# A vision tower's attention: the scaling of the probabilities goes from GpSimd to VectorE, as two operations with a scalar for each row

## The reference, cut to what matters

```python
scale = HEAD_DIM ** (-0.5)
attn = jnp.einsum('bhqd,bhkd->bhqk', q, k) * scale
attn = attn + jnp.einsum('bhqd,qkd->bhqk', q, r_p_k) * scale
attn = jax.nn.softmax(attn, axis=-1)
out = jnp.einsum('bhqk,bhkd->bhqd', attn, v)
out = out + jnp.einsum('bhqk,qkd->bhqd', attn, r_p_v)
return out.transpose(0, 2, 1, 3).reshape(b, n, QKV_DIM) @ proj_w.T + proj_b
```

## Time and profile before

| | us |
|---|---|
| median of 3 runs (4234.64 to 4243.27) | 4240.48 |
| the profiled execution | 4242.51 |
| its span | 4240.8 |
| TensorE busy in it | 4025.1 (95%) |
| VectorE busy | 2885.2 (68%) |
| ScalarE busy | 2497.5 (59%) |
| GpSimd busy | 1280.7 (30%) |

### The profile page before, as it was taken

One profiled execution on the slowest core, in us unless ns is written; L12 is line 12 of the kernel. 1 busy time (PEld: TensorE's weight loads), 2 busy tenths in 40 slices (PEclk: granted clock), 3 DMA queues, 4 the chain that ended last, 5 costly groups with the idle time before them and its releaser, 6 DMA issues. The chain is left out here.

```text
span 4240.8 us, 84769 instructions
## 1 busy us (share of the span) xinstructions
PE 4025.1 (95%) x28203; PEld 3938.8 (93%) x28203; DVE 2885.2 (68%) x7468; ACT 2497.5 (59%) x6686; POOL 1280.7 (30%) x1423
## 2 busy tenths in 40 slices
PE   4986799999999999999999999999999799999999
PEld 4886699999999999999999999999999799999999
DVE  4675566766666766676766676667666677777776
ACT  2554666666766666666676666666665344444443
POOL 1323322232232232223223223222222344444443
PEclk8998899999999999999999999999999899999999
DMA  8641100000000000000000000000000322222222
GB/s 188 141 114 48 36 1 1 1 25 1 2 24 2 1 2 24 1 1 24 1 1 25 1 1 2 24 1 1 13 1 1 92 93 93 93 91 87 82 90 90
DMA packets 88974, 161.67 MB, mean 38 GB/s; under 512 B 5706, under 2 KB 75937, under 8 KB 85055
## 3 DMA queue, kind: packets, MB, share of 16 engines
q1 hardware_dynamic: 85118, 152.66, 12.6%
q0 software_dynamic: 944, 2.42, 0.3%
q10 hardware_dynamic: 2576, 2.36, 0.2%
HBM read 127.82 MB, written 29.60 MB: 37 GB/s over the span
## 5 line engine op out<-in xcount | busy, mean ns | idle before, releaser
L637 POOL TENSOR_TENSOR att_prob<-att_prob,att_total 99x396 f32<-99x396 f32 x768 | 649.9, 846 | 2108.7 <-DVE att_total L869 2108.7
L877 DVE TENSOR_REDUCE att_npeak<-att_s 99x2 f32<-99x396 f32 x768 | 434.8, 566 | 449.4 <-PE att_s L1090 440.5
L718 ACT ACTIVATE att_probT<-att_t 99x396 f32<-99x396 f32 x768 | 384.1, 500 | 572.1 <-PE att_t L1056 566.7
L730 ACT ACTIVATE att_prob<-att_s,att_npeak 99x198 f32<-99x198 f32 x1536 | 636.6, 424 | 137.3 <-DVE att_npeak L877 135.4
L1073 PE MATMUL att_o<-att_probT,att_vx 99*96 99x198 f32 (+1 forms) x3072 | 653.5, 335 | 1.1 <-DVE att_rx L862 1.1
L1090 PE MATMUL att_s<-att_kx,att_qx 96*99 96x198 f32 (+1 forms) x3072 | 642.5, 332 | 5.2 <-DVE att_qx L821 2.2
L1278 POOL TENSOR_TENSOR ffn_hidden<-ffn_relu 128x384 f32<-128x384 f32 x462 | 425.3, 927 | 482.6 <-ACT ffn_relu L1307 480.6
L1090 PEld LDWEIGHTS att_s<-att_kx,att_qx 96*99 96x99 f32 (+1 forms) x3072 | 481.4, 166 | 12.4 <-issue 6.0
L1307 ACT ACTIVATE ffn_relu<-ffn_h 128x384 f32<-128x384 f32 x462 | 225.7, 489 | 448.4 <-PE ffn_h L1527 446.5
L1539 PE MATMUL ffn_y<-ffn_down,ffn_hidden 128*128 128x192 f32 x2772 | 487.3, 327 | 1.6 <-DVE ffn_hidden L1431 1.6
L1073 PEld LDWEIGHTS att_o<-att_probT,att_vx 99*96 99x96 f32 (+1 forms) x3072 | 469.5, 179 | 4.4 <-issue 1.4
(11 more groups left out here) (241 smaller groups left out, 8117.8 us busy)
## 6 DMA issues: line engine op xcount, KB each, us to landing
ffn_gates<-gate_rows SPq DMA_DIRECT2D x66, 768.0 KB, 5.5
tok_pixels<-in_x SPq DMA_DIRECT2D x24, 1568.0 KB
ffn_hid<-hidden SPq DMA_DIRECT2D x35, 288.0 KB, 3.0
att_xres<-hidden SPq DMA_DIRECT2D x8, 1188.0 KB
hidden<-att_xres SPq DMA_DIRECT2D x8, 1188.0 KB
ffn_acc<-hidden SPq DMA_DIRECT2D x33, 288.0 KB, 2.9
out_hidden<-ffn_acc SPq DMA_DIRECT2D x33, 288.0 KB, 2.4
hidden<-tok_rows SPq DMA_DIRECT2D x7, 1176.0 KB
```

The lines of the kernel that those rows point to most:

```text
L637: nc.gpsimd.tensor_tensor(prob[:, i % 2, :, :], prob[:, i % 2, :, :], view(total[:, i % 2, :], [[1, 2], [0, NTOK]]), ALU.mult).then_inc(pr ...
L718: nc.scalar.activation(probT[:, i % 2, :], t_bank[0:HALF, 0:2 * NTOK], ACT.Copy).then_inc(probT_made, 1)
L730: ins = nc.scalar.activation(prob[:, i % 2, h, :], s_bank[i % 2][0:HALF, h * NTOK:(h + 1) * NTOK], ACT.Exp, bias=npeak[:, i % 2, h:h + 1], ...
L877: nc.vector.tensor_reduce(npeak[:, i % 2, :], s_bank[i % 2][0:HALF, 0:2 * NTOK].rearrange("p (h k) -> p h k", h=2), AX.X, ALU.max, negate= ...
```

## The change

GpSimd's multiplication of the probabilities by the reciprocals (one operation with two tensors, 99 x 396) is taken out. VectorE gets `scaled`: it waits for its own reciprocal of the head before, and multiplies each half of the tile, 99 x 198, by a scalar for each row. That stands in VectorE's step n behind `inverted_sums` and behind `put_out`, and ahead of the step's jobs. The second of the two operations counts `probs`. GpSimd still adds the bias in the first 16 steps of a group, and now waits for `probs` instead of `inverted`.

```diff
                 def group(g, s):
                     for i in range(STEPS):
-                        pool.wait_ge(inverted, g * STEPS + i + 1)
-                        nc.gpsimd.tensor_tensor(prob[:, i % 2, :, :], prob[:, i % 2, :, :],
-                                                view(total[:, i % 2, :], [[1, 2], [0, NTOK]]), ALU.mult).then_inc(probs, 1)
                         if i < TILES:
+                            pool.wait_ge(probs, g * STEPS + i + 1)
                             if i == 0:
                                 pool.wait_ge(norm_made, (g + 1) * TURN)
                             ins = nc.gpsimd.tensor_tensor(xres[:, s, i, :], xres[:, s, i, :], pbias[:, :], ALU.add)
...
+                def scaled(n, i):
+
+                    j = i - 1
+                    dve.wait_ge(inverted, n - 1 + 1)
+                    for h in range(2):
+                        ins = nc.vector.tensor_scalar(prob[:, j % 2, h, :], prob[:, j % 2, h, :], total[:, j % 2, h:h + 1], None, ALU.mult)
+                    ins.then_inc(probs, 1)
+
...
                             inverted_sums(n, i)
                         if v != "first" or i >= 3:
                             put_out(n, i)
+                        if v != "first" or i >= 1:
+                            scaled(n, i)
                         for j in spreads[v][i]:
                             job(base, g, s, v, *j)
...
                     if i == STEPS:
                         inverted_sums(n, i)
+                        scaled(n, i)
                     put_out(n, i)
```

## The result

| | before | after |
|---|---|---|
| median of 4 runs each, us | 4241.0 | 4334.5 |
| ratio of the runs' times | 1 | 1.0226 (95%: 1.0211 to 1.0242) |
| span of the profiled execution | 4240.8 | 4329.6 |
| TensorE busy | 4025.1 | 4050.1 |
| VectorE busy | 2885.2 | 3285.7 |

The change made the kernel 93.5 us slower by the medians, 2.2%. 4324 was forecast, with 4272 to 4352 as the range. GpSimd's work halved, VectorE's grew by 400 us, and both mattered only through TensorE, whose matmuls are the same.

What follows compares the result with a forecast made beforehand. TensorE was taken as the bound. Seven groups' 66.5 us and the last group's 16.5 made 83 us on the span of 4240.8, so 4324 us; the range of 8 in 10 was 4272 to 4352.

Steps and rivals of the forecast that it cites:

- steps 74 to 82: Steps of a group where the next tokens are turned and VectorE is already the bound: 2.8 us lost a group.
- The way of 0.635 us behind L862: Scaled tile ready 0.585 us behind L862's end, plus 0.05 to the weight load: transposes can start 0.635 behind it.
- VectorE's time of 0.53 a step: What VectorE's line loses each step to the two scalings: the middle between 0.47 and 0.58 us.
- Unit ends: Steps 12 to 15 and the ends at 28 and 60: 0.9 us of VectorE's time plus 0.44 later transposes, 1.35 each.
- 42 to 47: Steps where the next group's statistics stand too: 1.63 us idle against 3.2 added, plus 0.44, so 2.0 us lost.
- the tail: Last group's 17 final steps with hardly any jobs: seven lose 0.93 us each, five some 0.5 each, 9 us.
- rival A: VectorE's added time is absorbed, only the longer chain to the transposes counts: 4281 us, range 4266 to 4300; chance 0.18.
- seven groups of 9.5 us: Every group but the last loses 9.5 us over its listed stretches, 66.5 us in all.
- The floor of 2.9: Loop from transpose load over weighing and copies to scaling: 2.26 plus 0.635, 2.9 us a step where rows show 1.97.
- (D): The work stays hidden, VectorE's idle time is used everywhere: within 0.2% of 4240 us; chance 0.04.
- (B): Late jobs free banks late, the ring of four empties, ScalarE gets peaks late: 4345 to 4390 us; chance 0.14.
- (C): GpSimd's operation slows VectorE's while both run, so without it the kernel gets faster: 4210 us; chance 0.04.

## Why the prediction was right, point by point

- **What bounds the kernel.** TensorE, with VectorE in steps 74 to 82 alone. Both hold: taking VectorE work out moved just these steps, up to what the clock did at a group's end.
- **The removed part.** GpSimd's operation was no bound, only a way of 0.98 us. Right as far as the runs go: a longer way alone cost 85 us. No run takes the operation away without putting work elsewhere.
- **The two operations.** Forecast 0.32 us with starts 0.235 apart; measured 0.321 and 0.24. The row taken for it, one scalar for each row at 192 columns, was the right one.
- **The way of 0.635 us behind L862.** Measured 0.64 in the step shown. The "0.93 or so" that the prediction puts between the reciprocal and the end of the copies runs from the reciprocal's start; from its end it is 1234.30 - 1233.51 = 0.79. No term of the sum uses it.
- **VectorE's time of 0.53 a step** was mis-sized. Where a job or the peaks follow, the next operation starts only when the second scaling has ended: 1258.12 + 0.56, then 1258.70. That makes 0.59. Where statistics follow, which read SBUF, the next one overlaps:

```profile
1386.62 0.56 DVE L874 TENSOR_SCALAR att_prob<-att_prob,att_total 99x198 f32<-99x198 f32 x2
1387.09 0.35 DVE L898 BATCH_NORM_STATS2 att_stat<-att_xres 99x6 f32<-99x192 f32 x1
```

  By the rule of the Trainium skill that the prediction weighed ("VectorE: DVE Perf Modes", section "Two Vector instructions with no wait between them"), the trace agrees in both cases: a reader of PSUM that starts in another quadrant than the last one is held, a reader of SBUF in the same quadrant isn't. All 271 operations of L819 and L846 that stand behind the scalings start 0.03 us after their end, all 49 of the statistics (L898, L903) some 0.08 to 0.09 before it. Its 0.58 was the better end of the range, and by its 10 us the sum would have been 4334. That this is the measured time is chance: it would make an ordinary group 10.9 us, which lost 10.0, and the rest of what was measured lies in places that the sum doesn't have (below).
- **Unit ends, 42 to 47, 74 to 82, the tail.** The forecast was 1.35, 2.0, 2.8 and 9 us. The unit ends were taken 0.2 too high, the other two stretches 0.3 too low. The end of the sixth unit (steps 92 to 95) has no term; it costs most of the 0.6 us of steps 83 to 95. The last group got 15.1 in place of 16.5. The split of a unit end (0.9 of VectorE's time, 0.44 of the way) was wrong in its parts: alone, the time takes 0.6, and the way takes 0.33 us when it is 0.44 long and 1.1 to 1.3 when it is 0.98. The rest of VectorE's lag seems to be worked off in the light steps behind, as rival A had it; its price for the whole was still wrong.
- **The step that was missed** is "seven groups of 9.5 us", and a term for TensorE's clock. The sum has 83 us for the attention, 93.9 were measured. The ordinary groups are 0.5 us dearer each, 3.5 in seven; the first group costs 6.6 us more than an ordinary one, the third's end 2.2 more, and the last group 1.4 less than forecast. In the first group three things come together. The first is 3.6 us in its steps 2 to 14. Its first unit has no jobs of the kind "last" of a pair before, so its steps have little TensorE work and meet the same floor as the tail. In the timeline of before two of its transpose loads stand 2.46 us apart:

```profile
511.23 0.51 PEld L1056 LDWEIGHTS att_t<-att_ident,att_prob 99*99 99x99 f32 x4
...
513.69 0.42 PEld L1056 LDWEIGHTS att_t<-att_ident,att_prob 99*99 99x99 f32 x3
```

  The second row is cut short by the window's end. In the timeline of the changed kernel the same two stand 2.82 apart, each behind a wait for L874:

```profile
508.70 0.42 PEld L1065 LDWEIGHTS att_t<-att_ident,att_prob 99*99 99x99 f32 x4 [0.35 <-DVE att_prob L874]
...
511.52 0.42 PEld L1065 LDWEIGHTS att_t<-att_ident,att_prob 99*99 99x99 f32 x4 [0.45 <-DVE att_prob L874]
```

  The floor of 2.9 was in the text, but was applied to the tail only. The second is 2.1 us in steps 15 and 16, where TensorE waited 3.0 us for a bank that VectorE frees (L819), before 2.2, and then ran longer at the lower clock. The third is 1.0 us in step 82, where the clock fell behind a wait of 2.0 us.
- **The clock.** In the profiled execution of before the granted clock fell at two places of the attention, at steps 15 and 16 of the first group and at the fifth group's end. In that of the changed kernel it fell at five: these two, step 82 of the first group, the third group's end, and step 90 of the last. Windows behind the stand at the third group's end and behind the one in the last group's step 90, of the kernel before (two rows) and of the changed one (two rows):

```profile
1537.00:1541.00 4.00, 4.00 (x28) 3.98 (x29) 1.57 (x4) 1.68 (x6) 0.85 (x1) 1.00 0.04 10
3263.00:3268.00 5.00, 5.00 (x36) 4.97 (x35) 4.17 (x11) 2.63 (x10) 1.69 (x2) 1.00 0.02 3
1571.00:1575.00 4.00, 4.00 (x21) 3.88 (x20) 1.65 (x5) 1.31 (x5) 0.00 (x0) 0.57 0.01 4
3350.00:3355.00 5.00, 4.91 (x23) 4.30 (x22) 2.52 (x7) 1.31 (x5) 0.00 (x0) 0.72 0.00 0
```

  The third number from the end is the granted clock: 1.00 is the full one, 0.57 and 0.72 mix it with the lower level. TensorE does fewer instructions in the same time. Each fall follows a stretch in which the weight loads stood idle: 2.6 us at the third group's end (1.6 before), 2.0 us in the last group's step 90 (1.4 before). The step behind the third group's end took 5.29 us where the one behind the second's took 3.72. By such step lengths the clock makes 1.3 us in steps 15 and 16, 1.0 in step 82, 1.6 at the third group's end and some 1.5 in the last group: some 5 of the 93.9 us, an estimate. Waiting as long doesn't always bring the fall: step 82 of the second group waited 2.04 us at full clock. Only one execution of each kernel was profiled, so how regularly the clock falls at these places is open.
- **Rivals.** (A), the lag absorbed, and (D) fall with the 58.5 and 64 us that VectorE's time costs with a short way and with GpSimd's. (B), banks freed late, is small: between 600 and 3050 us TensorE's matmuls waited 4.4 us for L846, in two waits at the ends of the third and fifth group (1.3 for L848 before, one wait), and in the first group 3.0 us for L819 where it was 2.2. (C), VectorE gains from GpSimd's silence: L846 (L848 before) takes 552 ns on average where it took 553. The Trainium skill ("SBUF — State Buffer", section "Who interferes with whom") has a port pair that the two engines share; for VectorE's readers of PSUM no effect of it is seen here.

```profile
PE att_s L1099 <- DVE att_xres L846: 4.4, 2, 2.3
...
L846 DVE TENSOR_TENSOR att_xres<-att_p,att_xres 99x384 f32<-99x384 f32 x330 | 169.1, 552 | 4.7
```

(The second row is from the list of groups of the same window.)

- **The range.** Its ends, 4272 and 4352, aren't A's middle (4281) and B's beginning (4345), as the prediction says, but some 8 us outside them. The measured 4334.5 lies inside either.
- **Two late places.** The 2.2 us more at the end of the third group, and some 2.2 us in the last group's steps 90 and 91 that the floor doesn't explain, are the longer idle stretches and the lower clock named above. At the third and at the fifth group's end the program's loop over pairs of groups turns; before lost 1.5 us at the one and 3.5 at the other against the other groups' ends, the changed kernel 3.7 and 3.4. In the last group TensorE waited 1.8 us there for L836, which stands behind the scalings in VectorE's line, and before 1.2 for L838. Why TensorE stands still at the loop's turns is open.

## What to carry to other kernels

A helper engine that is idle for 70% of the time can still be the right place for a step: ask not how long the step takes there, but where in the receiving engine's line it would stand, and what stands ahead of it. Three quantities gave the forecast: the distance at which the consumer already follows (0.19 us at a unit's end, 1.06 in a light step), the idle time of the receiving engine stretch by stretch, and the length of the loop that the new order closes, as a floor for every short step. Apply the last to all short steps, the start-up ones too, and look at the granted clock behind every stretch in which the bounding engine comes to stand longer than before. And where an engine is the bound for a short stretch only, moving its work in that stretch pays even onto an engine three times slower.

## What the hardware showed that I had not expected

- GpSimd is slower here with a scalar for each row than with two tensors: 786 ns for 99 x 198 and one scalar, 1007 ns for 99 x 192 with two scalars and two operations, against 592 ns for two tensors of 99 x 192 and 846 ns for 99 x 396. The rows are from the kernel with the row scalars on GpSimd (first two) and from the one with the normalisations on GpSimd:

```profile
L640 POOL TENSOR_SCALAR att_prob<-att_prob,att_total 99x198 f32<-99x198 f32 x1536 | 1188.4, 786 | 1609.1 <-DVE att_total L872 1609.1
L645 POOL TENSOR_TENSOR att_xres<-att_xres,att_pbias 99x192 f32<-99x192 f32 x128 | 75.8, 592 | 0.0
```

```profile
L639 POOL TENSOR_SCALAR att_norm<-att_xres,att_mv,att_sd 99x192 f32<-99x192 f32 x84 | 83.8, 1007 | 27.1 <-ACT att_x L699 27.1
```

- On VectorE a second row scalar with a second operation costs time too: 0.229 us from start to start with one of each at 192 columns, 0.29 with two (L787: one takes 0.376 us, two in a row 0.67). Which of the two it is, scalar or operation, no run tells apart.
